# Macaron block on one core: PSUM banks divided by step in the first and last stage, projections in eight pieces

## The reference

```
ffn(h):  logits = h @ router.T + router_bias          # 64 experts
         s = softmax(logits); keep the 8 largest
         return h * sum(kept) + kept_dense @ expert_bias
attn(h): q = h @ Wq.T (32 heads of 32), k, v = h @ Wk.T, h @ Wv.T (8 heads of 32)
         rope on q and k; scores causal; of each row the 205 largest scores are kept (all, where fewer)
         softmax over those, times v, @ Wo.T
x = x + 0.5 * ffn(layernorm(x))
x = x + attn(layernorm(x))
x = x + 0.5 * ffn(layernorm(x))
```

## Time and profile before

| what | value |
|---|---|
| median of three executions | 4730.14 us (4722.13 to 4741.39) |
| profiled execution, time | 4739.29 us |
| its span, first to last instruction | 4737.5 us |
| granted TensorE clock, mean over the span | 0.843 |
| PE, DVE, ACT, POOL busy | 74%, 67%, 57%, 43% of the span |
| first projection matmul of the first stage | 55.47 us |
| first matmul of the middle stage | 830.70 us |
| first projection matmul of the last stage | 4233.60 us |

### The profile page before, as it was taken

The page is one execution under the profiler, slowest core; times in us unless marked ns, Lnnn a source line. Parts: engine busy times, 40 slices in busy tenths (PEclk is TensorE's granted clock), DMA queues, the critical chain, the costliest instruction groups (busy, mean ns, idle before and its releaser), DMA issues. The chain is left out here.

```text
span 4737.5 us, 56552 instructions
## 1 busy us (share of the span) xinstructions
PE 3524.3 (74%) x16248; PEld 1649.4 (35%) x16248; DVE 3173.2 (67%) x6104; ACT 2688.0 (57%) x4577; POOL 2023.6 (43%) x5916
## 2 busy tenths in 40 slices
PE   5777775677868757787885678888567888857776
PEld 2333332233323323333332233333233333324443
DVE  2444444688988758888884888887488888822222
ACT  0111111688858757886885688887478888820000
POOL 1121211655535755554575554456565445620000
PEclk8777776688989878898997789989779999978887
DMA  2111111100001010000100100010010000011111
GB/s 97 42 52 43 51 40 44 34 11 11 9 6 21 16 30 12 11 9 7 21 16 19 24 11 9 9 21 14 19 26 11 9 9 11 15 72 53 54 40 40
DMA packets 221534, 124.04 MB, mean 26 GB/s; under 512 B 187940, under 2 KB 206628, under 8 KB 221092
## 3 DMA queue, kind: packets, MB, share of 16 engines
q1 hardware_dynamic: 221092, 119.36, 8.9%
HBM read 76.28 MB, written 42.99 MB: 25 GB/s over the span
## 5 line engine op out<-in xcount | busy, mean ns | idle before, releaser
L868 PE MATMUL banks<-pT,v_sb 128*65 128x512 f32 x2176 | 1186.3, 629 | 34.9 <-ACT oT L972 33.4
L957 ACT ACTIVATE pT<-banks 128x512 f32<-128x512 f32 x1088 | 637.7, 592 | 641.3 <-PE banks L840 634.9
L816 PE MATMUL banks<-k_sb,q_sb 128*128 128x512 bf16 (+3 forms) x1280 | 515.5, 403 | 388.5 <-DVE sc L1121 355.0
L1144 DVE MAX8 near<-keys 128x8 f32<-128x256 f32 (+14 forms) x480 | 653.4, 1361 | 16.5
L948 ACT ACTIVATE junk<-sc,t_all 128x256 fp8e4<-128x256 f32 (+14 forms) x480 | 599.2, 1249 | 31.9 <-DVE sc L1121 30.1
L948 ACT ACTIVATE junk<-sc,tiny 128x256 fp8e4<-128x256 f32 (+14 forms) x480 | 595.5, 1246 | 36.5 <-DVE sc L1129 36.2
L948 ACT ACTIVATE junk<-sc,tt 128x256 fp8e4<-128x256 f32 (+14 forms) x480 | 598.4, 1247 | 1.4 <-POOL tt L1013 0.8
L834 PE MATMUL banks<-q_sb,k_sb 128*128 128x512 bf16 x1088 | 447.0, 411 | 146.4 <-DVE fb L1298 124.7
L1121 DVE TENSOR_SCALAR_CACHE_REDUCE sc<-banks 128x1024 f32<-128x1024 f32 (+7 forms) x512 | 501.3, 980 | 52.1 <-PE banks L821 30.0
L1129 DVE TENSOR_SCALAR sc<-sc,tt 128x256 f32<-128x256 f32 (+14 forms) x480 | 360.5, 814 | 241.6 <-POOL tt L1034 241.5
L818 PE MATMUL banks<-k_sb,q_sb 96*128 96x512 bf16 (+3 forms) x1280 | 504.8, 404 | 0.0
(11 more groups left out here) (247 smaller groups left out, 5469.8 us busy)
## 6 DMA issues: line engine op xcount, KB each, us to landing
q_sb<-scratch_qk SPq DMA_DIRECT2D x896, 32.0 KB, 1.9
scratch_qk<-parts SPq DMA_DIRECT2D x16, 960.0 KB, 3.7
a_x<-in_x SPq DMA_DIRECT2D x16, 512.0 KB, 3.2
scratch_x<-a_x SPq DMA_DIRECT2D x16, 512.0 KB, 2.6
scratch_attn<-o_sb SPq DMA_DIRECT2D x128, 64.0 KB, 1.6
c_xn<-scratch_attn SPq DMA_DIRECT2D x16, 512.0 KB, 3.6
c_x<-scratch_x SPq DMA_DIRECT2D x16, 512.0 KB, 4.5
out<-c_x SPq DMA_DIRECT2D x16, 512.0 KB, 2.6
```

The lines of the kernel that those rows point to most:

```text
L816: nc.tensor.matmul(r_slot(n)[:, j:j + wj], q_sb[:, p % QS, 0, h, :], k_sb[:, group[p] % 2, 0, col:col + wj], start=True, stop=False)
L868: nc.tensor.matmul(psum[0:VP, 6, :], v_sb[:, group[p] % 2, kb, :], pT[:, n % PTS, :], start=(kb == 0), stop=(kb == blocks[p] - 1)).then_in ...
L957: nc.scalar.activation(pT[:, tn % PTS, :], psum[:, 4 + n % 2, :], ACT.Exp, scale=SCALE)\
L1144: v.max(near[:, h, :], z).then_inc(sm["key"], 1)
```

## The change

The banks are divided by step. First stage: banks 0 and 1 serve the ffn steps and the second transposes of every tile; banks 2 to 4 and 5 to 7 serve projections, q and k transposes, key moments and y, in turns by tile parity. Last stage: banks 0 to 3 (two per parity) serve the input transposes and the projection, banks 4 to 7 the ffn steps. The logits now lie in the bank of the first transposes, the mix transpose in the one behind it. The projection steps become eight pieces, one for each 128 rows of the contraction, each with a `yield` of its own. TensorE's wait for the deviation of tile t-2 moves from a tile's first step to its first projection piece, and new waits stand for the buffers that are now shared (hTcopy of the tile before; in the last stage xsum and x1 of tile t-2). The load of x is issued apart from those of rope and tab, which have a semaphore of their own. Periods and offsets change with it. y becomes one matmul for each group, over 128 contraction rows and 4 x 33 columns: moments16 gets an axis for the four heads, holds zeros off the diagonal blocks (one memset at the start), and is filled by four copies of 32 partitions. VectorE reads y in three pieces of up to 12 heads in place of four of 8.

```diff
-A_PERIOD, C_PERIOD = 42.0, 27.0
+A_PERIOD, C_PERIOD = 38.0, 26.0
+PAIR = 3
...
+def banks(psum, first, width):
+    return psum[:, first:first + -(-width // BANK), :].rearrange("p b n -> p (b n)")[:, 0:width]
...
+        b.ffn_bank = lambda t: 0
+        qkv_bank = lambda t: 2 + 3 * (t % 2)
-        rot = sb("rot", [P, U, H + HKV, HD])
+        rot = sb("rot", [P, 2, H + HKV, HD])
-        moments16 = sb("moments16", [P, U, HKV, VW], BF16)
+        moments16 = sb("moments16", [P, U, HKV, REP, VW], BF16)
...
+                nc.vector.memset(moments16[:, :, :, :, :], 0.0)
... SP, first stage
-                        yield -40
+                        yield -12
+                        if t >= U:
+                            sp.wait_ge(sm["h"], t - U + 1)
+                            sp.wait_ge(sm["x1out"], 16 * (t - U + 1))
+                        sp.dma_start(b.x[:, t % U, :], x_dram[rows, :]).then_inc(loaded[t % U], 16)
+                        yield 26
+                        sp.wait_ge(sm["x1"], t + 1)
+                        sp.dma_start(dram["x1"][rows, :], b.x[:, t % U, :]).then_inc(sm["x1out"], 16)
+                        yield 30
... guess, vout and out of tile t-U are waited for here, then rope and tab are loaded
... TensorE, first stage
-                        yield 6
-                        if t >= 2:
-                            pe.wait_ge(sm["deviation"], t - 1)
-                        yield from ffn_tensor(nc, pe, t, sm, b, 0)
-                        yield 29
-                        transpose8(nc, pe, t, sm["h"], t + 1, b, 4 * (t % 2) + 2, sm["hT"])
-                        yield 33
-                        pe.wait_ge(sm["hTcopy"], 2 * t + 2)
-                        pe.wait_ge(sm["x1"], t + 1)
+                        yield 7
+                        if t:
+                            pe.wait_ge(sm["hTcopy"], 2 * t)
+                        yield from ffn_tensor(nc, pe, t, sm, b, 1)
+                        yield 31
+                        transpose8(nc, pe, t, sm["h"], t + 1, b, b.ffn_bank(t), sm["hT"])
                         for c in range(DC):
+                            yield 35 + c * A_PERIOD / DC
+                            if c == 0:
+                                pe.wait_ge(sm["hTcopy"], 2 * t + 2)
+                                if t >= 2:
+                                    pe.wait_ge(sm["deviation"], t - 1)
...
-                        yield 58.5
+                        yield 81
... q and k transposes
-                        yield 61
+                        yield 85
... key moments
-                        yield 73
+                        yield 96
...
                         for g in range(HKV):
-                            for r in range(REP):
-                                q = slice(r * HD, (r + 1) * HD)
-                                last = nc.tensor.matmul(b.psum[:, 4 * (t % 2) + r, g * VW:(g + 1) * VW], parts[q, t % U, 0, g, :],
-                                                        moments16[q, t % U, g, :], start=True, stop=True)
+                            at = g % PAIR * REP * VW
+                            last = nc.tensor.matmul(b.psum[:, qkv_bank(t) + g // PAIR, at:at + REP * VW],
+                                                    parts[:, t % U, 0, g, :],
+                                                    moments16[:, t % U, g, :, :].rearrange("p r d -> p (r d)"),
+                                                    start=True, stop=True)
... ScalarE, first stage: 8 -> 9, 31 -> 33, 57 -> 79, 62 -> 83 (the third bank's copies first), 68 -> 90
... GpSimd, first stage: 59 -> 80, 83 -> 106
... VectorE, first stage: rope 54 -> 75, left 66 -> 87, low and moments 70 -> 92, y sums 75 -> 98
-                        nc.vector.tensor_copy(moments16[:, t % U, :, :], moments[:, t % U, :, :]).then_inc(sm["momcopy"], 1)
+                        for r in range(REP):
+                            q = slice(r * HD, (r + 1) * HD)
+                            nc.vector.tensor_copy(moments16[q, t % U, :, r, :], moments[q, t % U, :, :]).then_inc(sm["momcopy"], 1)
... last stage
+        b.ffn_bank = lambda t: 4 + 2 * (t % 2)
+        proj_bank = lambda t: 2 * (t % 2)
... TensorE, last stage
                         yield 0
                         if t >= 2:
-                            pe.wait_ge(sm["x1"], t - 1)
+                            pe.wait_ge(sm["xsum"], t - 1)
-                        transpose8(nc, pe, t, loaded[t % U], 32 * (t // U + 1), b, 4 * (t % 2) + 2, sm["aT"])
-                        yield 4
-                        pe.wait_ge(sm["aTcopy"], 2 * t + 2)
+                        transpose8(nc, pe, t, loaded[t % U], 32 * (t // U + 1), b, proj_bank(t), sm["aT"])
                         for c in range(DC):
+                            yield 6 + c * C_PERIOD / DC
+                            if c == 0:
+                                pe.wait_ge(sm["aTcopy"], 2 * t + 2)
...
-                        yield 26
-                        yield from ffn_tensor(nc, pe, t, sm, b, 20)
+                        yield 39
+                        if t >= 2:
+                            pe.wait_ge(sm["x1"], t - 1)
+                        yield from ffn_tensor(nc, pe, t, sm, b, 33)
... VectorE 19 -> 32 and ffn at 33, GpSimd 23 -> 36, ScalarE ffn at 33, SP -25 -> -17 and 44 -> 57
```

More of the change, by code:

```diff
@@ L100, in ffn_vector @@
     dve.wait_ge(sm["logits"], t + 1)
-    link(nc.vector.max(b.top[:, t % U, :], b.psum[:, 4 * (t % 2) + 2, 0:E]))
+    link(nc.vector.max(b.top[:, t % U, :], b.psum[:, b.ffn_bank(t), 0:E]))
     nc.vector.tensor_scalar(b.small[:, t % U, 0:1], b.top[:, t % U, 0:1], -1.0, None, ALU.mult).then_inc(sm["negmax"], 1)
@@ L115, in ffn_vector @@
     dve.wait_ge(sm["mixed"], t + 1)
[L116 to L121 removed]
+    nc.vector.tensor_tensor(b.x[:, t % U, :], b.x[:, t % U, :], banks(b.psum, b.ffn_bank(t), 2 * BANK),
+                            ALU.add).then_inc(sm["x1"], 1)
+def banks(psum, first, width):
+    return psum[:, first:first + -(-width // BANK), :].rearrange("p b n -> p (b n)")[:, 0:width]
 def ffn_tensor(nc, pe, t, sm, b, at):
[L126 removed]
+    transpose8(nc, pe, t, sm["xn"], t + 1, b, b.ffn_bank(t), sm["xT"])
     yield at + 10
     pe.wait_ge(sm["xTcopy"], 2 * t + 2)
[L129 removed]
+    logits = b.psum[:, b.ffn_bank(t), 0:E]
     for c in range(DC):
@@ L134, in ffn_tensor @@
     pe.wait_ge(sm["mix"], t + 1)
-    nc.tensor.transpose(b.psum[0:E, 4 * (t % 2) + 3, 0:P], b.mix[:, t % U, :], b.eye[:, :]).then_inc(sm["mixT"], 1)
+    nc.tensor.transpose(b.psum[0:E, b.ffn_bank(t) + 1, 0:P], b.mix[:, t % U, :], b.eye[:, :]).then_inc(sm["mixT"], 1)
     yield at + 18
@@ L138, in ffn_tensor @@
     for j in range(2):
-        last = nc.tensor.matmul(b.psum[:, 4 * (t % 2) + j, :], b.mixT[:, t % U, :], b.ebias[:, j * BANK:(j + 1) * BANK],
+        last = nc.tensor.matmul(b.psum[:, b.ffn_bank(t) + j, :], b.mixT[:, t % U, :], b.ebias[:, j * BANK:(j + 1) * BANK],
                                 start=True, stop=True)
@@ L155, in ffn_scalar @@
     act.wait_ge(sm["xT"], t + 1)
-    copy_xT(nc, t, b, 4 * (t % 2), sm["xTcopy"])
+    copy_xT(nc, t, b, b.ffn_bank(t), sm["xTcopy"])
     yield at + 14.5
     act.wait_ge(sm["negmax"], t + 1)
-    nc.scalar.activation(b.e64[:, t % U, :], b.psum[:, 4 * (t % 2) + 2, 0:E], ACT.Exp, bias=b.small[:, t % U, 0:1],
+    nc.scalar.activation(b.e64[:, t % U, :], b.psum[:, b.ffn_bank(t), 0:E], ACT.Exp, bias=b.small[:, t % U, 0:1],
                          accum_out=b.small[:, t % U, 1:2]).then_inc(sm["expd"], 1)
@@ L310, in phase_a @@
             loaded = [ctx2.enter_context(nc.semaphore(f"a_load{t}")) for t in range(U)]
+            angles = [ctx2.enter_context(nc.semaphore(f"a_angles{t}")) for t in range(U)]
             with nc.Block() as block:
@@ L587, in tile @@
                         act.wait_ge(sm["aT"], t + 1)
-                        copy_xT(nc, t, b, 4 * (t % 2) + 2, sm["aTcopy"])
-                        yield 28
+                        copy_xT(nc, t, b, proj_bank(t), sm["aTcopy"])
+                        yield 41
                         act.wait_ge(sm["proj"], t + 1)
-                        yield from ffn_scalar(nc, act, t, sm, b, 20)
+                        yield from ffn_scalar(nc, act, t, sm, b, 33)
                     staggered(tile, C_PERIOD)
@@ L607, in tile @@
                     def tile(t):
-                        yield 19
+                        yield 32
                         dve.wait_ge(loaded[t % U], 32 * (t // U + 1))
                         dve.wait_ge(sm["proj"], t + 1)
-                        link(nc.vector.tensor_tensor(b.x[:, t % U, :], b.x[:, t % U, :], bank2(b.psum, 4 * (t % 2)), ALU.add))
-                        yield 20
-                        yield from ffn_vector(nc, dve, link, t, sm, b, 20)
+                        nc.vector.tensor_tensor(b.x[:, t % U, :], b.x[:, t % U, :], banks(b.psum, proj_bank(t), D),
+                                                ALU.add).then_inc(sm["xsum"], 1)
```

(3 more changed lines are left out.)

92 lines of the change are left out of this document (45 added, 47 removed).

## The result

The changed kernel takes 4493.09 us (median of 4 runs, 4489.11 to 4498.07) against 4728.58 us of the kernel before (4 runs): a ratio of 0.9499, 95% interval 0.9477 to 0.9522. The profiled execution took 4494.27 us, its span is 4492.4 us, its granted clock 0.873. The prediction was 4480, the range 4430 to 4550.

The account below looks back on a forecast made before the run. No engine is full: serial tiles leave TensorE waiting, then at half clock. First stage -113.2 and last stage -136.7 give -249.9 on 4739.29, so 4489.4 profiled and 4480 as median; own range 4445 to 4515, wider 4430 to 4550.

Parts of the forecast that it names:

- The sum: Whole kernel: first stage -113.2 and last stage -136.7, together -249.9 us, with the middle stage untouched.
- The walk of the first stage: First stage, TensorE's order over one period: 36.3 us at one clock, 40.2 with clock losses, bounds 36.3 and 43.
- the wait of 0.98: First stage, ahead of the router: TensorE waits 0.9 us for ScalarE's two copies.
- 4.28 for h: First stage, after c7: pieces cover only part of VectorE's path behind y, so TensorE is idle 4.3 us.
- the cold transposes: First stage, behind the wait for h: the clock falls there and the transposes take 0.93 us more.
- the cold start: First stage, c0 and c1 partly at 1.2 GHz: 2.1 us taken, where bursts before paid 2.6 to 3.3.
- The second fall: Clock loss around the first stage's router: 0.9 us booked, bounds 0 and 2.5; rival, every period in both stages: 4547, chance 0.2.
- GpSimd's 2.1 us beside an idle VectorE: First stage, six GpSimd steps between statistics and h: 2.1 us without VectorE contention; 4.3 would make the period 38.5.
- the two long steps: First stage before the change: two of GpSimd's six steps take 1.28 and 1.50 us while VectorE subtracts left.
- Moments: First stage: eight larger matmuls replace 32, taken 0.5 us; copies +0.9 and reads -0.2 on VectorE; no gain booked.
- the last burst: End of the first stage: the last projections carry tile 14's steps and cold start, 25.4 against 23.9 us, +1.5.
- the stage's tail: End of the first stage: three more moment copies, +0.9 us.

Follow-up runs that it names:

- the one-run kernel: Changed kernel with the first stage's eight projection pieces issued in one run at offset 35: 4721.61 us, +228.5 on the changed kernel's 4493.09.
- the contention kernel: Changed kernel with two more, unused VectorE additions of 128x1024 between aggregation and normalization of the last stage, beside GpSimd's rstd steps: 4535.59 us, +42.5.
- the one with y behind c5: Changed kernel with y sums moved behind h, the router behind piece c3 and y's offset 98 in place of 96: 4409.70 us, -83.4.
- the last stage in one run: Changed kernel with the last stage's eight projection pieces issued in one run at offset 6: 4635.95 us, +142.9.

## Why the prediction was right

- *The sum.* Predicted -249.9 on the profiled execution, measured 4739.29 - 4494.27 = -245.0. First stage -111.4 (predicted -113.2), last stage -139.7 (-136.7), middle stage +6.0 (0), which is within its scatter. Against the prediction the stages are off by +1.8, -3.0 and +6.0, which partly cancel. Of the last stage's 3.0, 2.7 are 14 periods of 21.41 in place of 21.6. By the medians the change is -235.5. The 13 us between 4480 and the median 4493 are mostly the step from execution to median: the profiled execution of the kernel before lay 9 us above its median, that of the changed kernel 1 us above.
- *The walk of the first stage* held to a tenth: the wait of 0.98 (predicted 0.9), 4.28 for h (4.3), copy waits 1.18 and 0.36, no wait ahead of y but 0.68 for tile 14. c0 of tile 0 to c0 of tile 15 is 598.3 us (53.77 to 652.05) against 596.3 predicted, its first period 34.9 against 33.5 (two cold bursts, 1.5 and 2.9 us), its 14 later ones 40.24 each against 40.2. The warm walk deserves the tenth; the 40.24 owes some of it to luck, since in the three other kernels with this first stage the same 14 periods are 40.15 to 40.63. That it is the cover which gives this is shown by the one-run kernel (+225 us in this stage), that the y sums ahead of x1 make the wait by the kernel that moves them.
- *The clock.* +0.93 for the cold transposes was right; the cold start cost 1.5 to 3.0, a mean of 2.3 (booked 2.1). The second fall was booked at a mean of 0.9 and called a rival where it comes each time. It came in six of 14 periods, 1.4 to 3.1 us each: 13.5 us in all, 1.0 a period. The three other kernels with the same first stage show it in five, seven and eight of 14. The 0.9 was a choice between bounds of 0 and 2.5 and its nearness is luck; the picture of a small loss in each period was wrong, as a period has none of it or 1.4 us and more. Piece c3 ahead of the router removes the fall from c3 and c4 but moves it behind the wait for y; it is gone from both places only where that wait and the one for h are gone too. In the last stage it never came, as forecast.
- *GpSimd's 2.1 us beside an idle VectorE* is 2.19; the contention kernel shows the other price, 3.67, so the reading of the earlier trace rows is shown and not only argued. Of the two long steps that the prediction names, both put beside left, the 1.28 stands there; the 1.50 (L181, from 428.74) stands beside low (L488, from 428.71), the other subtraction.
- *Moments.* y takes 0.64 us warm (0.5 taken); the part alone saves nothing (+8 us on the kernel before). The sum was right to book no gain, by the rows alone: at the same place behind cold transposes 32 small matmuls take 0.42 us and eight large ones, which stream as many columns in all (1056), 1.09. The Trainium skill (TensorE: Matmul & The Clock Gate, Part 3) has it that four matmuls in separate row groups cost about what one does. The rows agree in kind, with a factor of 2.6 and not four; no run here parts this from other reasons.
- *Terms that were off*, each by little: the last burst +2.4 (1.5 booked), with the wait of 0.68 for y in it; the stage's tail +1.5 (0.9 booked); its first projection 1.7 us sooner than before, not booked, since x no longer waits for rope and tab at the start; x lands in 4.2 us and not 3.2, with no effect.

## What to carry to other kernels

When one tile's steps form a chain, cut the long independent work of the next or the last tile into pieces and lay one behind each link of the chain; walk the queue of each engine. In the changed kernel the waits that are left came out to a tenth of a microsecond; where a queue was not walked (the moment copies in the kernel with the router behind c3, rope in the one with y behind c5), the miss was 1.7 and 2.1 us of wait. Then look at the queue that stands behind the last uncovered link: here work that nothing needed so soon (the deviation of an older tile) stood ahead of work that TensorE waited for. Moving it was worth 63 us, and moving it, splitting it and placing router and y one piece later 119. Price every remaining TensorE wait twice, once for its length and once for the clock that it may bring down.

## What the runs showed of the hardware that was not expected

- A few waits of 1 to 2.5 us in a row were enough to bring TensorE to half clock even with transposes and router matmuls between them (1.23 and 2.42 us, with the last stage in one run): that kernel, without the 7 us wait, had the same mean period of 30.73 us as one with it.
- The clock can fall in some periods of one loop only: every second one with a wait of 2.49 us, none with 0.81 (last stage); five to eight of 14 behind the router in four kernels with the same first stage. In the last stage of the kernel before every third projection burst took 16.5 us and the others 14.00. Means over periods hide it, a list of the same row through all periods shows it.
- GpSimd's steps of 0.2 to 0.6 us stretch to 1.1 to 1.4 us beside a VectorE addition of 128x1024 with two SBUF inputs, one step for each addition (contention kernel: 0.22 to 1.08, 0.57 to 1.40).
